# Own terms of a graph layer in SBUF instead of PSUM, and eight low parts moved behind the last one-hots

## The chip, the cores and the metric

The kernel runs on one core of a Trainium2 chip. The metric is the device time in microseconds of one execution. Inputs and outputs are as in the reference; nothing is computed on the host.

## The reference

There are 1250 nodes with 512 features, 20,000 directed edges, and a self loop for each node. A first layer (GIN) sums neighbours, adds the node's own term, and goes through two linear maps with batch norm; a second layer (a hidden map of 256) sums neighbours again. Each is followed by a residual sum and a layer norm.

```
agg = segment_sum(x[src], dst, N)
h = (1 + eps) * x + agg                       # "own term" and sum
h = relu(batch_norm(h @ W1 + b1, g1, be1))    # 512 -> 1024
h = relu(batch_norm(h @ W2 + b2, g2, be2))    # 1024 -> 512
x = layernorm(x + (x + h))
h = relu(x @ V1 + c1) @ V2 + c2               # 512 -> 256 -> 512
x = layernorm(x + (h + segment_sum(h[src], dst, N)))
```

## The kernel before, in words

The five engines have each a program written out by hand in one order, tied by counting semaphores; a wait names the count at which the instruction behind it may go, and everything behind it on that engine waits too. Products in float32 are made of fp32r operands, a high part and a low part (value minus high part), so a product is three matmuls: high by high, high by low, low by high.

The adjacency matrix is never read. VectorE writes one-hot matrices for 50 destination nodes at a time (`one_hots`, lines 850 and 853, 25 groups), TensorE multiplies them into a block of the adjacency (`build`, line 1212), and ScalarE copies the block to `AT` (`group_out`, line 572). TensorE's aggregate (line 1232) multiplies the features by `AT`: twelve sums, numbered i = 0 to 11, four feature blocks for each of three column chunks of 250, 500 and 500 nodes (so sums 0 to 3 have 250 columns, 4 to 11 have 500). Sum i stands in PSUM bank 2 + i % 6. Sums 0 to 3 are accumulated in group slots 0 to 14, sums 4 to 7 in slots 15 to 24, in between the builds, and sums 8 to 11 behind the last group, one after another.

A finished sum goes through three steps. `h0_own(i)` on VectorE (line 864) adds (1 + eps) x to it, and writes back into the bank. `h0_high(i)` on ScalarE (line 597) copies it to `h0h` as fp32r. `h0_low(i)` on VectorE (line 871) writes the difference to `h0l`. For the first eight sums these stand 2, 3 and 5 groups behind the group that ends the sum (`OWN_LAG`, `HIGH_LAG`, `LOW_LAG`), between VectorE's one-hots, and the last of them right behind the last group.

Then VectorE's program goes on: the parameters out of PSUM (line 957), four small multiplications for `gains` (line 961), and then, interleaved, the self loops (`loops(k)`, line 966, k = 0 to 9, an int16 addition into `half_out`) and the steps of sums 8 to 11: loops 0, 1, 2, own 8, loops 3, low 8; loops 4, 5, own 9, loops 6, low 9; loops 7, 8, own 10, loops 9, low 10; own 11, low 11. ScalarE's program beside it: `halve` 0 to 3 (line 642, `AT` rows to int16 in one of four `half_out` buffers), high 8, halve 4, 5, 6, high 9, halve 7, 8, 9, high 10, high 11. SyncE stores each `half_out` behind its `loops` (line 403); `halve(k)` for k of 4 and more waits until the store of k - 4 has landed, since it writes the same buffer. GpSimd at this time subtracts for the low parts of W1 (line 486, eight instructions, two tensors in SBUF read, one written), which begin when the last block of `AT` is copied.

TensorE goes from the last sum straight to the first linear map (line 1296): for output tile t, column chunks c = 0, 1, 2, four feature blocks, three matmuls each. For t = 0 chunk c waits until h0l_set has reached 7, 8 and 12. Tile t = 2 waits until batch norm and activation of tile 0 have freed its banks.

Of the kernel before, what the change touches and what calls it, by code (L numbers as in the profile page):

```python
# [6 lines left out]
F32 = mybir.dt.float32  # L7
# [4 lines left out]
ACT = mybir.ActivationFunctionType  # L12
AX_X = mybir.AxisListType.X

P = 128
# [4 lines left out]
def cdiv(a, b):  # L20
    return -(-a // b)


def gnn_kernel(nc, x, src, dst, eps, w1, b1, g1, be1, w2, b2, g2, be2, lw1, lb1, lw2, lb2, out, a_spill):
# [14 lines left out]
    DT, HT, LT = D // P, H // P, L // P  # L39
# [6 lines left out]
    NG = NW // WG  # L46
# [10 lines left out]
    CH = [(0, 250), (250, 750), (750, 1250)]  # L57
# [5 lines left out]
    with ctx:  # L63
        def sem(name):
            return ctx.enter_context(nc.semaphore(name))
# [10 lines left out]
        R_H0 = R_AT + cdiv(NT * N * 4, 64) * 64  # L76
# [6 lines left out]
        def at(name, shape, dt, offset):  # L83
            return nc.alloc_sbuf_tensor_at(name, shape, dt, offset=offset)
# [13 lines left out]
        def small(n):  # L98
            o = small_n[0]
            small_n[0] += n  # L100
            assert small_n[0] <= SMALL
            return small_t[:, o:o + n]

        xs = at("xs", [P, NT, D], F32, R_W + 32 * KB - NT * D * 4)
        xT = at("xT", [P, DT, N], F32, R_XT + XSHIFT)
# [7 lines left out]
        h0h = [at(f"h0h{c}", [P, DT, c1 - c0], F32R, R_H0 + 2 * DT * c0 * 4) for c, (c0, c1) in enumerate(CH)]  # L113
        h0l = [at(f"h0l{c}", [P, DT, c1 - c0], F32R, R_H0 + DT * (c0 + c1) * 4) for c, (c0, c1) in enumerate(CH)]

        w1s = at("w1s", [P, HT, DT * P], F32, R_W)
        wl = at("wl", [P, HT, DT * P], F32R, R_W)
        wh = at("wh", [P, HT, DT * P], F32R, R_W + 16 * KB)
# [71 lines left out]
        eps_in, asked, eps1 = small(1), small(1), small(1)  # L190
# [32 lines left out]
        ps = ctx.enter_context(nc.psum_tensor("ps", [P, 8, BANK], F32))  # L223
# [6 lines left out]
        x_turned, xT_set, h0_own_set = sem("x_turned"), sem("xT_set"), sem("h0_own_set")  # L230
# [5 lines left out]
        const, ident_set = sem("const"), sem("ident_set")  # L236
# [11 lines left out]
        h0_sum, h0h_set, h0l_set = sem("h0_sum"), sem("h0h_set"), sem("h0l_set")  # L248
# [23 lines left out]
        RING = 6  # L272

        def zbank(t, n):
            return 2 + 3 * (t % 2) + n
# [60 lines left out]
        NI = len(CH) * DT  # L336
# [8 lines left out]
            for j in range(per):  # L345
                slot_units[slots[j * len(slots) // per]].append(units[c * per + j])
        tail_units = units[(len(CH) - 1) * per:]
        OWN_LAG, HIGH_LAG, LOW_LAG = 2, 3, 5
        EARLY = CHG[0]
        cols_at = {6: half + 2, 7: half + 3, 11: half + 4}  # L350
        turn_at = {6: half + 2, 7: half + 3, 12: half + 4}
# [6 lines left out]
        def h0_after(g):  # L358
            return [i for i, k in slot_units[g] if k == NT - 1] if g >= 0 else []
# [200 lines left out]
        def _(act):  # L560
# [30 lines left out]
            def h0_high(i):  # L591
                c, d = divmod(i, DT)
                c0, c1 = CH[c]
                act.wait_ge(h0_own_set, i + 1)
                if i == 0:
                    act.wait_ge(const, 9)
                nc.scalar.activation(h0h[c][:, d, :], ps[:, 2 + i % 6, 0:c1 - c0], ACT.Copy).then_inc(h0h_set, 1)

            for k in range(half):
                x_high(k)  # L600
# [198 lines left out]
        def _(v):  # L799
            n = [0]  # L800

            def link(ins):
# [11 lines left out]
                                           in1=src_i[0:ER, :], op0=ALU.mult, op1=ALU.add).then_inc(pair_set, 1)  # L814
            nc.vector.scalar_tensor_tensor(out=edge_row[0:ER, :], in0=win_row[0:ER, :], scalar=dst_f[0:ER, 0:1],
                                           in1=below[0:ER, :], op0=ALU.is_gt, op1=ALU.subtract).then_inc(rowsel, 1)
# [19 lines left out]
            for c in range(2):  # L836
# [7 lines left out]
                                                    in1=keyT[:, :, c], op0=ALU.add, op1=ALU.subtract))  # L844
# [12 lines left out]
            def h0_own(i):  # L857
                c, d = divmod(i, DT)
                c0, c1 = CH[c]
                v.wait_ge(h0_sum, i + 1)  # L860
                if i == 0:
                    v.wait_ge(xT_set, NT)
                o = ps[:, 2 + i % RING, 0:c1 - c0]
                nc.vector.scalar_tensor_tensor(out=o, in0=xT[:, d, c0:c1], scalar=eps1[:, 0:1], in1=o,
                                               op0=ALU.mult, op1=ALU.add).then_inc(h0_own_set, 1)

            def h0_low(i):
                c, d = divmod(i, DT)
                c0, c1 = CH[c]
                v.wait_ge(h0h_set, i + 1)  # L870
                nc.vector.tensor_tensor(h0l[c][:, d, :], ps[:, 2 + i % 6, 0:c1 - c0],
                                        h0h[c][:, d, :].bitcast(F32), ALU.subtract).then_inc(h0l_set, 1)

            v.wait_ge(const, 7)
# [8 lines left out]
            with v.If(bad == 0):  # L883
                for g in range(EARLY, NG):
                    one_hots(g)
                    if g in low_at:
                        x_low(low_at[g])
                    for i in h0_after(g - OWN_LAG):
                        h0_own(i)
                    for i in h0_after(g - LOW_LAG):  # L890
                        h0_low(i)
                for g in range(NG, NG + LOW_LAG):
                    for i in h0_after(g - OWN_LAG) if g - OWN_LAG < NG else []:
                        h0_own(i)
                    for i in h0_after(g - LOW_LAG):
                        h0_low(i)
            with v.Else():


                v.wait_ge(const, 9)  # L900
                for k in low_at.values():
                    x_low(k)
                v.wait_ge(AT_set, EARLY)
                nc.vector.memset(gen_0[:, :], 0.0).then_inc(gen_zero, 1)
                nc.vector.tensor_copy(gen_src[0:ER, :], src_i[0:ER, :]).then_inc(gen_copied, 1)
                with v.Fori(0, NT) as h:
                    with v.Fori(0, EC) as f:
                        v.wait_ge(gen_copied, h * 4 + 1)

                        v.wait_ge(gen_used, h * (EC + 1) + f + 1)  # L910
                        nc.vector.tensor_scalar(gen_s[0:ER, :], iota2[0:ER, :, 0], gen_src[0:ER, bass.ds(f, 1)],
                                                None, ALU.is_equal).then_inc(gen_hot, 1)
                        nc.vector.tensor_scalar(gen_d[0:ER, :], nodes[0:ER, :], dst_f[0:ER, bass.ds(f, 1)],
                                                None, ALU.is_equal).then_inc(gen_hot, 1)
                    v.wait_ge(gen_sum, h + 1)
                    for c, (c0, c1) in enumerate(CH):
                        nc.vector.tensor_copy(AT[:, bass.ds(h, 1), c0:c1],
                                              ps[:, 2 + c, None, 0:c1 - c0]).then_inc(gen_copied, 1)
                    nc.vector.tensor_scalar(gen_src[0:ER, :], gen_src[0:ER, :], -float(P), None,
                                            ALU.add).then_inc(gen_copied, 1)  # L920
                v.wait_ge(gen_copied, 4 * NT + 1)
                nc.vector.memset(n_out[:, :], 0.0).then_inc(AT_set, NG - EARLY)
                for i in range(NI - DT):
                    h0_own(i)
                    h0_low(i)


            def row_stats(k, part):
# [233 lines left out]
        def _(pe):  # L1162
# [53 lines left out]
            def aggregate(i, k):  # L1216
                c, d = divmod(i, DT)
                c0, c1 = CH[c]
                o = ps[:, 2 + i % RING, 0:c1 - c0]
                if k == 0:  # L1220
                    pe.wait_ge(AT_set, CHG[c])
                    if i >= RING:
                        pe.wait_ge(h0l_set, i - RING + 1)
                    elif i >= DT:
                        pe.wait_ge(xT_set, NT)
                    else:
                        pe.wait_ge(xT_set, half)
                if i == 0:
                    pe.wait_ge(xl_set, k + 1)
                r = rows[k]  # L1230
                for j, part in enumerate((xh, xl)):
                    last = mm(o, part[0:r, k, d * P:d * P + P], AT[0:r, k, c0:c1], start=(k == 0 and j == 0),  # L1232
                              stop=(k == NT - 1 and j == 1))
                if k == NT - 1:
                    last.then_inc(h0_sum, 1)
# [51 lines left out]
            for t in range(HT):  # L1287
                pe.wait_ge(w1l_set, t + 1)
                if t >= 2:
                    pe.wait_ge(act_set, 2 * t - 2)  # L1290
                for c, (c0, c1) in enumerate(CH):
                    if t == 0:
                        pe.wait_ge(h0l_set, max(DT * (c + 1), 7 + c))
                    for d in range(DT):
                        for j, (w, h) in enumerate(((wh, h0h), (wl, h0h), (wh, h0l))):
                            last = mm(ps[:, zbank(t, c), 0:c1 - c0], w[:, t, d * P:d * P + P], h[c][:, d, :],  # L1296
                                      start=(d == 0 and j == 0), stop=(d == DT - 1 and j == 2))
                        if c == len(CH) - 1 and d == DT - 1:
                            last.then_inc(z_sum, 1)
# [137 lines left out]
```

## Time and profile before

| what | value |
|---|---|
| median of 3 runs | 249.21 us (248.9 to 249.46) |
| the profiled execution, its own time | 249.12 us |
| its span, first to last instruction | 247.1 us |
| TensorE matmul busy | 231.4 us, 94% of the span |
| VectorE, ScalarE, GpSimd busy | 156.2, 134.2, 87.5 us |
| share of TensorE in the chain that ended last | 69% |
| mean granted TensorE clock | 0.992 |

Times in a trace are from the first instruction of the span. The profiled execution's own time is 2.0 us longer than its span, which is what lies around the span. A busy share says little about a stretch: what counts in a stretch is which wait ends last there. "Idle before" of an instruction is the time for which its engine stood still ahead of it.

### The profile page before, as it was taken

The numbers are of one execution on the slowest core, as the hardware profiler recorded it, in microseconds if no ns is written. First come the engines' busy times: TensorE is split into PE (matmuls) and PEld (weight loads), VectorE is DVE, ScalarE is ACT, GpSimd is POOL, SyncE is SP. The second block draws the span as 40 slices with busy tenths as digits, with TensorE's granted clock in tenths as the row PEclk, the third lists the DMA queues.
The fourth block names the chain that finished last, engine by engine and source line by source line (L and its number), as shares of the span: only waits on it lengthen the run. The fifth ranks groups of instructions, "written<-read, shape, count | busy, mean of one in ns | idle before, by whom it ended". The sixth has DMA issues, their size and how long they took to land.

```text
span 247.1 us, 3901 instructions
## 1 busy us (share of the span) xinstructions
PE 231.4 (94%) x1454; PEld 197.8 (80%) x1454; DVE 156.2 (63%) x362; ACT 134.2 (54%) x233; POOL 87.5 (35%) x83
## 2 busy tenths in 40 slices
PE   1859999999999999999999999999999999999991
PEld 1738988777888878888888888888889997888970
DVE  2778999873965343555554326164786899796274
ACT  0936865664677067444445504457461639935373
POOL 7500000006900007565654500423366459701241
PEclk9997999999999999999999999999999999999999
DMA  5287600000086401111000098503209920000334
GB/s 176 88 265 198 163 0 3 1 3 3 3 311 232 157 1 45 42 42 45 0 0 0 0 201 153 106 3 69 38 9 164 209 78 3 0 0 0 131 126 161
DMA packets 32322, 19.96 MB, mean 81 GB/s; under 512 B 21927, under 2 KB 27084, under 8 KB 32302
## 3 DMA queue, kind: packets, MB, share of 16 engines
q1 hardware_dynamic: 31868, 19.47, 29.7%
q8 instruction: 13, 0.21, 0.4%
q0 software_dynamic: 160, 0.13, 0.2%
q10 hardware_dynamic: 274, 0.09, 0.1%
q14 instruction: 7, 0.06, 0.1%
HBM read 8.51 MB, written 5.92 MB: 58 GB/s over the span
## 4 chain that ended last, share of the span: by engine, by line
PE 69%; DVE 12%; ACT 7%; DMA 5%; issue 2%; POOL 2%; SPq 1%; DVEq 0%; POOLq 0%; ACTq 0%
PE ps L1296 19%; PE ps L1232 17%; PE ps L1313 11%; PE ps L1359 9%; PE ps L1377 6%; PE ps L1326 3%; DMA plane_T<-planes 2%; PE ps L1212 2%; DVE small_t L943 2%; DVE xT L987 2%; DVE hot_s L850 2%; DMA pairs<-pair 1%; ACT planes L718 1%; DMA run<-pairs,start_i 1%; ACT a L681 1%
## 5 line engine op out<-in xcount | busy, mean ns | idle before, releaser
L943 DVE BATCH_NORM_STATS2 small_t<-ps 128x6 f32<-128x500 f32 (+1 forms) x36 | 21.6, 599 | 39.1 <-PE ps L1296 25.6
L1232 PE MATMUL ps<-AT,xh 128*128 128x500 f32 (+2 forms) x120 | 42.7, 367 | 0.2 <-ACT AT L572 0.2
L1232 PE MATMUL ps<-AT,xl 128*128 128x500 f32 (+2 forms) x120 | 40.9, 352 | 0.0
L1296 PE MATMUL ps<-h0h,wh 128*128 128x500 f32 (+1 forms) x96 | 33.9, 353 | 0.2 <-ACT a L681 0.2
L1296 PE MATMUL ps<-h0h,wl 128*128 128x500 f32 (+1 forms) x96 | 33.9, 353 | 0.0
L1296 PE MATMUL ps<-h0l,wh 128*128 128x500 f32 (+1 forms) x96 | 33.8, 352 | 0.0
L491 POOL TENSOR_TENSOR wl<-w2s,wh 128x512 fp32r<-128x512 f32 x8 | 11.1, 1382 | 44.4 <-ACT wh L692 44.4
L486 POOL TENSOR_TENSOR wl<-w1s,wh 128x512 fp32r<-128x512 f32 x8 | 10.1, 1296 | 45.8 <-ACT AT L572 45.8
L1232 PEld LDWEIGHTS ps<-AT,xh 128*128 128x128 f32 (+1 forms) x120 | 22.6, 188 | 3.2 <-ACT AT L572 0.4
L1232 PEld LDWEIGHTS ps<-AT,xl 128*128 128x128 f32 (+1 forms) x120 | 22.7, 189 | 2.7
L1313 PE MATMUL ps<-a1h,wh 128*128 128x500 f32 (+1 forms) x96 | 23.7, 355 | 0.0
L1313 PE MATMUL ps<-a1h,wl 128*128 128x500 f32 (+1 forms) x96 | 23.5, 353 | 0.0
L1313 PE MATMUL ps<-a1l,wh 128*128 128x500 f32 (+1 forms) x96 | 23.4, 353 | 0.0
L572 ACT ACTIVATE AT<-ps 128x500 fp32r<-128x500 f32 x25 | 14.7, 589 | 15.4 <-PE ps L1212 15.4
L850 DVE TENSOR_TENSOR hot_s<-iota,loT 128x1280 bf16<-128x1280 bf16 x25 | 20.5, 819 | 2.4 <-PE ps L1212 2.2
L1359 PE MATMUL ps<-A,uh 128*128 128x512 f32 (+3 forms) x60 | 20.5, 357 | 0.0
L1296 PEld LDWEIGHTS ps<-h0h,wh 128*128 128x128 f32 x96 | 18.1, 188 | 3.0 <-issue 0.6
L1359 PE MATMUL ps<-A,ul 128*128 128x512 f32 (+3 forms) x60 | 20.3, 354 | 0.0
L1296 PEld LDWEIGHTS ps<-h0l,wh 128*128 128x128 f32 x96 | 18.0, 188 | 2.5
L1296 PEld LDWEIGHTS ps<-h0h,wl 128*128 128x128 f32 x96 | 18.1, 188 | 2.4
L495 POOL TENSOR_TENSOR a1l<-a,a1h 128x1250 fp32r<-128x1250 f32 x7 | 18.8, 2681 | 0.0
L666 ACT ACTIVATE small_t<-small_t 128x1 f32<-128x1 f32 x12 | 3.5, 295 | 27.7 <-DVE small_t L944 27.6
(150 smaller groups left out, 509.2 us busy)
## 6 DMA issues: line engine op xcount, KB each, us to landing
turns<-half_out SPq DMA_DIRECT2D x10, 320.0 KB, 2.2
out<-x SPq DMA_DIRECT2D x9, 256.0 KB
w1s<-in_L_gnn_W SPq DMA_DIRECT2D x4, 512.0 KB, 7.0
w2s<-in_L_gnn_W SPq DMA_DIRECT2D x8, 256.0 KB, 2.8
xs<-in_x SPq DMA_DIRECT2D x1, 1280.0 KB, 6.4
xs<-in_x SPq DMA_DIRECT2D x1, 1024.0 KB
lws<-in_L_gnn_W SPq DMA_DIRECT2D x1, 512.0 KB, 3.9
lw2s<-in_L_gnn_W SPq DMA_DIRECT2D x1, 512.0 KB, 4.3
```

The costliest lines, as they stand in the source:

```text
L486: nc.gpsimd.tensor_tensor(wl[:, t, :], w1s[:, t, :], wh[:, t, :].bitcast(F32), ALU.subtract).then_inc(w1l_set, 1)
L491: nc.gpsimd.tensor_tensor(wl[:, t, :], w2s[t % W2R][:, :], wh[:, t, :].bitcast(F32), ALU.subtract).then_inc(w2l_set, 1)
L495: nc.gpsimd.tensor_tensor(a1(a1l, t), a32[t % 2][:, :], a1(a1h, t).bitcast(F32), ALU.subtract).then_inc(a1l_set, 1)
L572: nc.scalar.activation(AT[:, :, g * WG * WIN:(g + 1) * WG * WIN].rearrange("p k (w d) -> p k w d", w=WG), ps[:, g % 2, 0:GCOLS].rearrange( ...
L850: nc.vector.tensor_tensor(hot_s[g % 2][:, :, :, :], iota2[:, None, :, :].broadcast_to([P, WG, P, 2]), loT[:, w, None, :].broadcast_to([P, ...
L943: link(nc.vector.bn_stats(stats[:, 6 * c:6 * c + 6], ps[:, zbank(t, c), 0:c1 - c0]))
L1232: last = mm(o, part[0:r, k, d * P:d * P + P], AT[0:r, k, c0:c1], start=(k == 0 and j == 0), stop=(k == NT - 1 and j == 1))
L1296: last = mm(ps[:, zbank(t, c), 0:c1 - c0], w[:, t, d * P:d * P + P], h[c][:, d, :], start=(d == 0 and j == 0), stop=(d == DT - 1 and j == 2))
L1313: last = mm(ps[:, zbank(t, c), 0:c1 - c0], w[:, k, (t - HT) * P:(t - HT + 1) * P], a1(a, k)[:, c0:c1], start=(k == 0 and j == 0), stop=(k ...
L1326: last = mm(u_at(k), x[:, d, P * k:P * k + r], w[:, d, :], start=(d == 0 and j == 0 and k % 2 == 0), stop=(d == DT - 1 and j == 2), skip_g ...
L1359: last = mm(v_at(i, m), (uh, ul)[j][0:r, k, m * P:m * P + P], a_rows(k)[0:r, c0:c1], start=(k == 0 and j == 0 and (m == 0 or v_banks[i][0] ...
L1377: last = mm(ps[0:r, y_banks[k % len(y_banks)], :], part[:, f:f + r], w[:, m, :], start=(m == 0 and j == 0), stop=(m == LT - 1 and j == 2))
```

## The change

`h0_own` writes its result to `h0f`, a float32 view in SBUF of the place of `h0l`. `h0_high` and `h0_low` read it from there, `h0_low` in place. The aggregate's wait for a free bank counts own terms and no longer low parts, and the first linear map has an added wait on own terms for its banks. The low parts 0 to 7 leave VectorE's loop over the groups and stand together behind own 7, ahead of the copy of the parameters. Sums 8 to 11 keep their order.

```diff
+        h0f = [at(f"h0f{c}", [P, DT, c1 - c0], F32, R_H0 + DT * (c0 + c1) * 4) for c, (c0, c1) in enumerate(CH)]
...
-        OWN_LAG, HIGH_LAG, LOW_LAG = 2, 3, 5
+        OWN_LAG, HIGH_LAG = 2, 3
...
                 act.wait_ge(h0_own_set, i + 1)
-                if i == 0:
-                    act.wait_ge(const, 9)
-                nc.scalar.activation(h0h[c][:, d, :], ps[:, 2 + i % 6, 0:c1 - c0], ACT.Copy).then_inc(h0h_set, 1)
+                nc.scalar.activation(h0h[c][:, d, :], h0f[c][:, d, :], ACT.Copy).then_inc(h0h_set, 1)
...
                 if i == 0:
                     v.wait_ge(xT_set, NT)
-                o = ps[:, 2 + i % RING, 0:c1 - c0]
-                nc.vector.scalar_tensor_tensor(out=o, in0=xT[:, d, c0:c1], scalar=eps1[:, 0:1], in1=o,
+                    v.wait_ge(const, 9)
+                nc.vector.scalar_tensor_tensor(out=h0f[c][:, d, :], in0=xT[:, d, c0:c1], scalar=eps1[:, 0:1],
+                                               in1=ps[:, 2 + i % RING, 0:c1 - c0],
                                                op0=ALU.mult, op1=ALU.add).then_inc(h0_own_set, 1)
...
                 v.wait_ge(h0h_set, i + 1)
-                nc.vector.tensor_tensor(h0l[c][:, d, :], ps[:, 2 + i % 6, 0:c1 - c0],
+                nc.vector.tensor_tensor(h0l[c][:, d, :], h0f[c][:, d, :],
                                         h0h[c][:, d, :].bitcast(F32), ALU.subtract).then_inc(h0l_set, 1)
...
                     for i in h0_after(g - OWN_LAG):
                         h0_own(i)
-                    for i in h0_after(g - LOW_LAG):
-                        h0_low(i)
-                for g in range(NG, NG + LOW_LAG):
-                    for i in h0_after(g - OWN_LAG) if g - OWN_LAG < NG else []:
+                for g in range(NG - OWN_LAG, NG):
+                    for i in h0_after(g):
                         h0_own(i)
-                    for i in h0_after(g - LOW_LAG):
-                        h0_low(i)
...
                 for i in range(NI - DT):
                     h0_own(i)
-                    h0_low(i)
+            for i in range(NI - DT):
+                h0_low(i)
...
                     if i >= RING:
-                        pe.wait_ge(h0l_set, i - RING + 1)
+                        pe.wait_ge(h0_own_set, i - RING + 1)
...
                     if t == 0:
                         pe.wait_ge(h0l_set, max(DT * (c + 1), 7 + c))
+                        pe.wait_ge(h0_own_set, 7 + c)
```

## Rows read from the trace of the kernel before

**Rows 1.** The page: busy time, share of the span and instructions.

```profile
PE 231.4 (94%) x1454; PEld 197.8 (80%) x1454; DVE 156.2 (63%) x362; ACT 134.2 (54%) x233; POOL 87.5 (35%) x83
```

**Rows 2.** The chain that ended last, in order of time: start, us, what.

```profile
59.44 18.38 PE ps L1232 x80
77.82 6.87 PE ps L1296 x36
...
91.68 41.27 PE ps L1296 x216
```

**Rows 3.** Windows view of the group loop: length, busy us of each engine, clock.

```profile
37.76:59.26 21.50, 21.50 (x172) 16.47 (x171) 15.26 (x31) 12.53 (x25) 1.19 (x1) 1.00 0.01 3
```

**Rows 4.** Timeline of VectorE from 43 to 81 us: start, us, instruction.

```profile
43.88 1.38 DVE L871 TENSOR_TENSOR h0l<-ps,h0h 128x250 fp32r<-128x250 f32 x4
...
50.12 0.67 DVE L871 TENSOR_TENSOR h0l<-ps,h0h 128x500 fp32r<-128x500 f32 x1
...
59.30 0.74 DVE L864 SCALAR_TENSOR_TENSOR ps<-xT,small_t,ps 128x500 f32<-128x500 f32 x1 [3.86 <-PE ps L1232]
59.95 1.43 DVE L871 TENSOR_TENSOR h0l<-ps,h0h 128x500 fp32r<-128x500 f32 x2
...
61.52 4.14 DVE L961 TENSOR_SCALAR gains<-small_t 128x8 f32<-128x8 f32 x4
65.69 2.83 DVE L966 TENSOR_TENSOR half_out<-half_out,ident 128x128 int16<-128x128 int16 x3
68.44 0.73 DVE L864 SCALAR_TENSOR_TENSOR ps<-xT,small_t,ps 128x500 f32<-128x500 f32 x1
...
80.11 0.68 DVE L871 TENSOR_TENSOR h0l<-ps,h0h 128x500 fp32r<-128x500 f32 x1 [0.66 <-ACT h0h L597]
```

**Rows 5.** Timeline of TensorE: the first matmul of chunk 2 of tile 0, and of tile 1.

```profile
81.79 0.39 PE L1296 MATMUL ps<-h0h,wh 128*128 128x500 f32 x1
...
84.52 0.28 PE L1296 MATMUL ps<-h0h,wh 128*128 128x250 f32 x1
```

**Rows 6.** Timeline of GpSimd behind the last group.

```profile
58.07 10.10 POOL L486 TENSOR_TENSOR wl<-w1s,wh 128x512 fp32r<-128x512 f32 x8 [45.80 <-ACT AT L572]
```

**Rows 7.** Timelines of VectorE and GpSimd where two instructions overlap, in two places.

```profile
139.51 1.46 DVE L982 TENSOR_TENSOR a1l<-a,a1h 128x1250 fp32r<-128x1250 f32 x1 [2.99 <-ACT a1h L701]
140.08 2.04 POOL L491 TENSOR_TENSOR wl<-w2s,wh 128x512 fp32r<-128x512 f32 x1 [2.71 <-ACT wh L692]
...
170.83 2.89 POOL L503 TENSOR_TENSOR xpl<-xT,xph 128x1250 fp32r<-128x1250 f32 x1 [8.17 <-ACT xph L709]
171.73 3.08 DVE L1002 TENSOR_TENSOR lw1l<-lws,lw1h 128x1024 fp32r<-128x1024 f32 x1 [3.40 <-ACT lw1h L728]
```

**Rows 8.** Groups by form, VectorE: busy us and mean ns of one.

```profile
L1033 DVE TENSOR_TENSOR xpl<-xT,xph 128x500 fp32r<-128x500 f32 x1 | 0.7, 671 | 0.0
L953 DVE TENSOR_SCALAR small_t<-gains,small_t 128x1 f32<-128x1 f32 x24 | 5.1, 214 | 1.0 <-DVE small_t L948 0.2
```

**Rows 9.** Timeline of SyncE's queue, and the landing times of line 403.

```profile
67.09 11.19 SPq L403 DMA_DIRECT2D turns<-half_out  x10
...
DMA to landing us min/median/max: 2.2/2.2/2.8
```

**Rows 10.** Timeline of ScalarE: halve 4.

```profile
69.69 1.24 ACT L642 ACTIVATE half_out<-AT 128x1250 int16<-128x1250 f32 x1
```

**Rows 11.** Timelines at 212 us: VectorE's first line 1104, GpSimd's two instructions beside it.

```profile
211.96 3.57 DVE L1104 SCALAR_TENSOR_TENSOR x<-b_all,small_t,x 128x512 f32<-128x512 f32 x1 [1.52 <-ACT x L747]
...
211.38 1.23 POOL L529 CAST A<-half_in 98x1250 fp32r<-98x1250 int16 x1
212.58 2.40 POOL L551 TENSOR_TENSOR lw2l<-lw2s,lw2h 128x1024 fp32r<-128x1024 f32 x1
```

**Rows 12.** Windows view of TensorE: length, PE busy, granted clock, DMA share, GB/s.

```profile
12.00:17.70 5.70, 2.51 (x29) 1.00 0.80 247
17.70:21.10 3.40, 3.38 (x40) 0.50 0.44 117
```

## The prediction

> **What bounds the kernel now.** The page comes first: TensorE is busy 94% of the span [rows 1], so a gain must come from a stretch in which TensorE waits. The windows view shows that there is none where the change takes work away: in the 21.50 us of the group loop in which low parts stand, TensorE is busy for 21.50 [rows 3]. The chain in order of time says the same for what follows: 80 matmuls of sums 8 to 11, then the 36 of tile 0 without a wait between them, then batch norm and activation of tile 0, and only when that has freed the banks the 216 of tiles 2 to 7 [rows 2]. From this the reader should keep two things. Up to 84.7 us only a wait that is new can move TensorE. And a wait ahead of the end of tile 0 is not made up for: tile 1 takes as long as tile 0, 6.9 us, and from tile 0's end at 84.7 to tile 2's start at 91.68 is 7.0 us, the chain's own length.
>
> The engine's timelines come next, for the margin. The last matmuls of tile 0, chunk 2, start at 81.79 [rows 5] and need low part 11, which ends at 80.11 + 0.68 = 80.79 [rows 4]. The margin is 1.0 us. Own 8 starts at 68.44, and from there to 80.79 own, high and low parts, halves and self loops wait for each other in turn, 12.35 us.
>
> **What it removes.** Four low parts of 250 columns (1.38 us) and two of 500 columns (0.67 each, the second like the one shown) leave VectorE's loop, 2.7 us [rows 4]. Low parts 6 and 7 were behind own 7 already. Gain: nothing, as TensorE had no wait there [rows 3], and VectorE itself then idles for 3.86 us ahead of own 7, which waits for the sum [rows 4]. The bounds are 0 and 0.5 us, the latter what a faster pitch of the matmuls could give (a rival, below). The bank waits that now count own terms were met long before. Writing the own term to SBUF, and reading it from there on ScalarE: no row shows the same form with the other memory; the nearest, a subtraction of 500 columns with all in SBUF, takes 0.671 us [rows 8] against 0.67 to 0.68 from PSUM [rows 4]. I take zero, with bounds of 0.1 us either way.
>
> **What it adds: eight low parts behind own 7, and now each reads two tensors in SBUF.** They stand ahead of the parameters, the four instructions of `gains`, self loops 0 to 2 and own 8. Alone they would be cheap. But GpSimd is at its eight subtractions, 58.07 to 68.17, 1.26 us each [rows 6], and the trace shows that such pairs exclude each other. At 171.73 a VectorE subtraction of 1024 columns, both inputs in SBUF, took 3.08 us; at the rate of the 500-column one (0.671) and the 1250-column one (1.46), 1.05 ns a column, it should take 1.2. It ended 1.09 us after GpSimd's instruction (170.83 + 2.89 = 173.72), so it stood until that was done. At 140.08 it is GpSimd that took 2.04 in place of 1.26, and ended 1.15 us after VectorE's [rows 7, 8]. The old low parts, with one input in PSUM, show nothing of this: two of them in 1.43 us while GpSimd worked [rows 4, 6].
>
> The Trainium skill (SBUF — State Buffer, § Who interferes with whom) states the rule: a VectorE instruction with two SBUF inputs takes its second one through the read interface that GpSimd reads by, and whichever comes second is blocked for the whole instruction. By this rule the low parts are new rivals of GpSimd, and without it they would cost the time of the case "no exclusion" below; these rows agree with it.
>
> Who goes next when both have a queue? `gains` needed 4.14 us for four tiny instructions, one per GpSimd instruction, and GpSimd still had work until 68.17: one got in behind each of GpSimd's [rows 4, 6]. I take this turn-taking. A blocked low part then ends 0.27 us (250 columns) or 0.53 us (500) after GpSimd's instruction, and the next of GpSimd's 1.15 us later:
> - GpSimd's second ends at 60.6. Four low parts of 250 with GpSimd's next behind each: 4 x 1.42 = 5.7, 66.3.
> - Two of 500 with GpSimd's seventh and eighth: 2 x 1.68 = 3.4, 69.7. GpSimd is done (its w1 parts are needed from 77.8 on, so its own delay costs nothing).
> - Two more of 500: 0.53 + 0.6, 70.8.
> - Parameters 0.2, and `gains` now unhindered, 4 x 0.25 by the 214 ns of line 953 and its gap [rows 8]: 72.0.
> - Self loops 0 to 2, 0.2 each (alone): loops 0 ends at 72.3, own 8 starts at 72.6, 4.2 late.
>
> What is queued behind it: high 8 when own 8 is done, 0.73 later, and halve 4, which was at 69.69 [rows 10]. It needs store 0 landed as well. The first store was issued at 67.09, 0.1 after loops 0, and lands 2.2 us later [rows 9]: now 72.4 + 2.2 = 74.6. So the store, not own 8, sets halve 4: 4.9 late. The rest of the 12.35 us shifts with it, low part 11 ends at 85.7, and TensorE, which can do chunks 0 and 1 and no more, waits 4.9 - 1.0 = about 4.0 us (rounding kept upward for the semaphore). SyncE's loads of W2, behind the stores in its queue, move from 78.4 to 83.3; ScalarE takes the first of them behind the activation of tile 0, which ended by 91.68 [rows 2], so they cost nothing.
>
> **What a stall costs beyond itself.** In 12.00 to 17.70 TensorE was busy for 2.51 of 5.70 us, and then the granted clock was 0.50 for 3.4 us, the 1.2 GHz level [rows 12]. The new gap of 4 us may bring the same, just ahead of the rest of tile 0. If 3.4 us at the half level are all work, 1.7 us are lost; if part of them falls into the gap, less. I take 1.5, with bounds 0 and 1.7.
>
> **Sum.** 249.12 (the profiled execution's own time, 0.1 below the median) + 4.0 + 1.5 = 254.6 us.
>
> **Rivals.**
> - *GpSimd first.* At 211.96 a VectorE instruction with two SBUF inputs took 3.57 us: it waited for a cast and for the subtraction that followed it too [rows 11]. If low part 0 had so to wait until 68.17: eight low parts unhindered, 0.27 + 3 x 0.35 + 4 x 0.6 = 3.7 (0.35 from 1.38 / 4, rows 4), to 71.9, `gains` to 73.1, loops 0 to 73.4, landing 75.7, halve 4 6.0 late, stall 5.0; with 0 to 1.7 of clock 254.1 to 255.8. Against it stands `gains`, in this very stretch.
> - *VectorE keeps its turn.* All eight in one go: 60.6 to 64.3, GpSimd's other six until 71.9. `gains` and two self loops wait for one each, own 8 at about 72.0, 3.5 late; store 0 landed in time. Stall 2.5: 251.6, with the clock 253.1. For it: low parts have no wait between them, `gains` had.
> - *No exclusion.* The low parts run from 59.95 to 63.7 beside GpSimd; `gains` still waits four times, to 68.2; loops 0 at 68.4 in place of 67.0, its store landed at 70.7, halve 4 1.0 to 1.2 late, stall 0.0 to 0.2: 249.1 to 249.3, no change. Rows 7 speak against it.
> - *Faster.* The loop's matmuls share PSUM with fewer readers and writers. A matmul of sums 8 to 11 takes 18.38 / 80 = 0.2298 us [rows 2], while the 12 of chunk 2, beside an almost idle VectorE, take (84.52 - 81.79) / 12 = 0.2275 [rows 5]; over the 160 long matmuls of sums 4 to 11 that is 0.4 us, 248.8. It decides only if halve 4 is at most 1.0 us late, hence only without exclusion.
>
> **Chances.** Turn-taking with the clock falling 0.42, without it (253.1) 0.13; GpSimd first 0.12; VectorE keeps its turn 0.15; no exclusion 0.08; faster 0.05; a stall longer than any of these, say by a store that lands after 2.8 us and two low clock stretches, 0.05. The range 251.6 to 256.2 holds the first four. What this kernel's timing can tell from no change is about 0.2%, 0.5 us: faster 0.05, same 0.08, slower 0.87.
>
> **What the profile after would show.** Low parts 0 to 7 on VectorE from 59.95 to about 70.8, some of them near 1.4 to 1.8 us long, and line 486 on GpSimd stretched beyond 10.10 us; `gains` at 0.2 to 0.4 us each; the first store at about 72.4; on TensorE a gap of about 4 us ahead of chunk 2 of tile 0, at 81.8, put down to the low part of line 871; perhaps a clock of 0.5 behind it; and from tile 2 to the end the same lengths as before. I am wrong if line 486 keeps its 1.26 us and the low parts their 0.4 and 0.67, or if the margin at 81.8 is larger than I read it.

## The result, and the profile after

The changed kernel takes 254.68 us (median of 5 runs) against 248.9 (median of 5) for the kernel before on the same chip; the ratio is 1.0241, 95% interval 1.020 to 1.028: slower by 2.4%. Forecast were 254.6 us and slower. One run of the changed kernel, 330.86 us, was disturbed and stands outside the ratio. In a second measurement on another chip the changed kernel takes 254.61 against 249.04, ratio 1.0245 (1.0206 to 1.0284).

The profiled execution took 257.7 us, 3 us more than the median. Most of that, some 2.5 us, has a cause ahead of the change, so it is set apart first; the rest, 0.9 us, is a longer stretch at the lower clock, shown further down. This is the piece of the changed kernel's chain that differs:

```profile
4.69 6.49 DMA pairs<-pair
```

The same transfer took 3.70 us in the kernel before's profile. Everything behind it in the profile below is late for that reason: own 7 starts at 61.62, 2.32 us after its place in [rows 4]. A second profiled execution of the changed kernel, 254.45 us, from the second measurement, had no such delay (the transfer took 3.63 us, own 7 started at 59.12), and the accounts below are made with it.

VectorE's timeline of the changed kernel, where [rows 4] show the one before:

```profile
61.62 0.73 DVE L863 SCALAR_TENSOR_TENSOR h0f<-xT,small_t,ps 128x500 f32<-128x500 f32 x1 [4.45 <-PE ps L1229]
62.27 10.86 DVE L871 TENSOR_TENSOR h0l<-h0f,h0h 128x250 fp32r<-128x250 f32 x8
73.05 0.18 DVE L954 COPY small_t<-ps 128x36 f32<-128x36 f32 x1
73.27 0.79 DVE L958 TENSOR_SCALAR gains<-small_t 128x8 f32<-128x8 f32 x4
74.09 0.70 DVE L963 TENSOR_TENSOR half_out<-half_out,ident 128x128 int16<-128x128 int16 x3
74.71 0.73 DVE L863 SCALAR_TENSOR_TENSOR h0f<-xT,small_t,ps 128x500 f32<-128x500 f32 x1
...
87.26 0.68 DVE L871 TENSOR_TENSOR h0l<-h0f,h0h 128x500 fp32r<-128x500 f32 x1 [0.69 <-ACT h0h L596]
```

The eight low parts take 10.86 us where the forecast reckons 3.7 for eight alone. `gains`, which waited for GpSimd four times (4.14 us), now takes 0.79: GpSimd is through by then. GpSimd's and SyncE's timelines, against [rows 6] and [rows 9]:

```profile
60.39 11.62 POOL L487 TENSOR_TENSOR wl<-w1s,wh 128x512 fp32r<-128x512 f32 x8 [45.68 <-ACT AT L573]
...
74.46 10.89 SPq L404 DMA_DIRECT2D turns<-half_out  x10
```

Line 487 is stretched from 10.10 to 11.62 us. The length of one, by the view of that line and of line 871 (ns min/median/max):

```profile
L487 POOL TENSOR_TENSOR wl<-w1s,wh x8: 1288/1465/1728, 60.4 to 70.3; 128x512 fp32r<-128x512 f32 x8
...
L871 DVE TENSOR_TENSOR h0l<-h0f,h0h x12: 667/1214/1767, 62.3 to 87.3; 128x500 fp32r<-128x500 f32 x8, 128x250 fp32r<-128x250 f32 x4
```

The shortest of GpSimd, 1288, is the length without a wait, and so is 667 for a low part of 500 columns; the longest are 1728 and 1767. The store and TensorE follow. First ScalarE's timeline, against [rows 10], then TensorE's, against [rows 5]:

```profile
75.47 0.62 ACT L596 ACTIVATE h0h<-h0f 128x500 fp32r<-128x500 f32 x1 [7.54 <-DVE h0f L863]
76.71 1.25 ACT L641 ACTIVATE half_out<-AT 128x1250 int16<-128x1250 f32 x1 [0.62 <-DMA turns<-half_out]
```

```profile
83.89 0.39 PE L1294 MATMUL ps<-h0l,wh 128*128 128x500 f32 x1
87.99 0.78 PE L1294 MATMUL ps<-h0h,wh 128*128 128x500 f32 x1 [3.71 <-DVE h0l L871]
```

Halve 4 is put down to the store, 0.62 us after high 8 was done. On TensorE the next matmul would start 0.23 after the one at 83.89, at 84.12; it starts at 87.99, a gap of 3.87 us, put down to a low part. Behind it the windows view shows the lower level of the clock, 1.2 GHz, and then the upper:

```profile
87.10:93.80 6.70, 5.81 (x16) 0.50 0.41 152
93.90:120.00 26.10, 26.10 (x139) 1.00 0.11 31
```

In the second profiled execution the chain from the low parts to the first map reads so, times from the start of its own span:

```profile
59.78 10.86 DVE h0l L871 x8
...
71.60 0.31 DVE half_out L963
...
71.97 2.23 DMA turns<-half_out
...
74.22 3.80 ACT half_out L641 x6
...
84.77 0.69 DVE h0l L871
...
85.50 52.63 PE ps L1294 x264
138.13 2.08 PE ps L1311 x11
```

Low parts, self loop 0, the store, halve 4 to 6, and so to low part 11: that is the forecast's path, engine by engine. The account: chunk 2 starts at 85.50 in place of 81.79, 3.71 later (a gap of 3.89 less 0.18 by which TensorE was early in this execution). From there to the second map it is 52.63 us, and 51.15 before (from 81.79 in [rows 5] to the end of the 216 matmuls in [rows 2], 132.94): 1.48 for the clock. Together 5.19; the spans differ by 252.4 - 247.1 = 5.3, the times by 254.45 - 249.12 = 5.3. Nothing of size is left for the rest of the kernel.

### The profile page after: what moved, and what is told of

It is laid out like the page before. It is cut to its first block, busy times and chain, and to the rows that moved or that the text cites. A ratio compares the mean times of both kernels' runs of the same rounds, so it can differ in the third digit from the quotient of the medians.

```text
span 255.7 us, 3902 instructions
## 1 busy us (share of the span) xinstructions
PE 233.9 (91%) x1454; PEld 199.3 (78%) x1454; DVE 157.6 (62%) x362; ACT 134.7 (53%) x233; POOL 89.0 (35%) x83
## 4 chain that ended last, share of the span: by engine, by line
PE 61%; DVE 17%; ACT 9%; DMA 8%; issue 2%; POOL 1%; SPq 1%; DVEq 0%
PE ps L1294 21%; PE ps L1311 11%; PE ps L1357 9%; PE ps L1229 9%; PE ps L1375 5%; DVE h0l L871 5%; ACT half_out L641 3%; PE ps L1324 3%; DVE hot_s L849 3%; DMA pairs<-pair 3%; DMA plane_T<-planes 2%; PE ps L1209 2%; DVE xT L984 2%; ACT planes L717 1%; DVE small_t L940 1%
## 5 line engine op out<-in xcount | busy, mean ns | idle before, releaser
L1294 PE MATMUL ps<-h0h,wh 128*128 128x500 f32 (+1 forms) x96 | 35.1, 365 | 3.7 <-DVE h0l L871 3.7
L1294 PE MATMUL ps<-h0h,wl 128*128 128x500 f32 (+1 forms) x96 | 34.9, 364 | 0.0
L1294 PE MATMUL ps<-h0l,wh 128*128 128x500 f32 (+1 forms) x96 | 34.9, 363 | 0.0
L487 POOL TENSOR_TENSOR wl<-w1s,wh 128x512 fp32r<-128x512 f32 x8 | 11.6, 1486 | 45.7 <-ACT AT L573 45.7
L1294 PEld LDWEIGHTS ps<-h0h,wh 128*128 128x128 f32 x96 | 18.9, 196 | 6.8 <-DVE h0l L871 4.1
L1294 PEld LDWEIGHTS ps<-h0l,wh 128*128 128x128 f32 x96 | 18.8, 195 | 2.7
L1294 PEld LDWEIGHTS ps<-h0h,wl 128*128 128x128 f32 x96 | 18.8, 196 | 2.6
```

The source lines that it names most:

```text
L487: nc.gpsimd.tensor_tensor(wl[:, t, :], w1s[:, t, :], wh[:, t, :].bitcast(F32), ALU.subtract).then_inc(w1l_set, 1)
```

## The experiments

Two theories of the lateness were to be told apart: the low parts and GpSimd's subtractions exclude each other since both inputs of a low part stand in SBUF; or it is the move alone, eight instructions in front of everything that sum 8 waits for. Beside them stand the terms of the sum: the store, the gap, the clock. The first four kernels ran on one chip, where the kernel before had a median of 249.49 (25 runs, from 248.7 to 252.25), the last four on another, median 249.04 (15 runs). Each profile's times count from its own start.

**GpSimd held back.** Line 485:

```diff
             pl.wait_ge(AT_set, NG)
+            pl.wait_ge(h0_own_set, 9)
```

> The changed kernel, with GpSimd's eight W1 subtractions held back until own 8 is done. Theory (VectorE's low parts and GpSimd's subtractions exclude each other, and that makes own 8 late): the eight low parts run from own 7 on in about 3.7 us at 0.41 and 0.67 us each, gains takes about 1 us, own 8 starts some 7 us earlier than in the changed kernel, TensorE has no gap ahead of chunk 2 of tile 0, time 248.9 (within 0.3) as the kernel before. Rival (it is the 3.7 us of low parts in front of own 8, whatever GpSimd does, with the store behind it): low parts keep their lengths of 0.9 to 1.8 us and the time stays near 254.4.

Measured: ratio 1.0028 (0.9983 to 1.0073), no difference from the kernel before; median 250.34, five of ten runs from 248.77 to 249.56 and five from 251.12 to 251.62 (the kernel before on this chip has two such clusters too, see the last section). VectorE's timeline:

```profile
60.15 3.76 DVE L872 TENSOR_TENSOR h0l<-h0f,h0h 128x250 fp32r<-128x250 f32 x8
63.83 0.19 DVE L955 COPY small_t<-ps 128x36 f32<-128x36 f32 x1
64.05 0.79 DVE L959 TENSOR_SCALAR gains<-small_t 128x8 f32<-128x8 f32 x4
...
65.49 0.73 DVE L864 SCALAR_TENSOR_TENSOR h0f<-xT,small_t,ps 128x500 f32<-128x500 f32 x1
...
66.90 1.28 DVE L872 TENSOR_TENSOR h0l<-h0f,h0h 128x500 fp32r<-128x500 f32 x1 [0.49 <-ACT h0h L597]
```

The same eight instructions at the same place take 3.76 us, not 10.86. Low part 8, now beside GpSimd, takes 1.28 in place of 0.68. TensorE has no gap ahead of chunk 2, and the whole loss is gone. But holding GpSimd back also takes `gains` from 4.14 to 0.79 us, about as much as the low parts add. So this does not yet show that the move by itself costs nothing, nor that two SBUF inputs are what makes it dear.

**One SBUF input.** Low parts 0 to 7 subtract from PSUM bank 1 in place of `h0f`, so that they are not those of the reference. The added wait, for the last block of `AT`, was met before they began:

```diff
-                nc.vector.tensor_tensor(h0l[c][:, d, :], h0f[c][:, d, :],
+                other = ps[:, 1, 0:c1 - c0] if i < NI - DT else h0f[c][:, d, :]
+                nc.vector.tensor_tensor(h0l[c][:, d, :], other,
                                         h0h[c][:, d, :].bitcast(F32), ALU.subtract).then_inc(h0l_set, 1)
...
+            v.wait_ge(AT_set, NG)
             for i in range(NI - DT):
```

> The changed kernel, with low parts 0 to 7 subtracting from a block of PSUM bank 1 in place of h0f: one SBUF input in place of two, same place, same size, same count; the low parts of these eight sums are then not those of the reference. Theory (exclusion by the second SBUF input): they take 0.41 and 0.67 us each though GpSimd works beside them, GpSimd keeps 1.26 us each, gains still waits four times, the first store is issued about 1.3 us later than before, TensorE's gap is 0 to 0.3 us, time 248.9 to 249.3. Rival (the move itself, 3.7 us of work ahead of gains and own 8, or SBUF as output): a gap of 2.5 to 4 us and 252 to 254.4.

Measured: ratio 1.0003 (0.9958 to 1.0048), no difference. Its profile, with the same slow first transfer as above and hence about 3 us late, on VectorE, GpSimd and TensorE:

```profile
63.19 3.73 DVE L872 TENSOR_TENSOR h0l<-ps,h0h 128x250 fp32r<-128x250 f32 x8
...
67.05 4.33 DVE L960 TENSOR_SCALAR gains<-small_t 128x8 f32<-128x8 f32 x4
...
61.30 10.06 POOL L487 TENSOR_TENSOR wl<-w1s,wh 128x512 fp32r<-128x512 f32 x8 [46.33 <-ACT AT L573]
...
84.80 0.39 PE L1296 MATMUL ps<-h0l,wh 128*128 128x500 f32 x1
85.31 0.50 PE L1296 MATMUL ps<-h0h,wh 128*128 128x500 f32 x1
```

This settles it. GpSimd works beside the low parts, at 10.06 us unhindered, and they are unhindered too, 3.73. One input's memory is different, with place, count, size and output the same. (The low parts are then no longer in place either. That being in place is what blocks is ruled out by [rows 7]: line 1002, which is not in place, stood until GpSimd was done.) `gains` waits its four times as before, 4.33 us. Reckoned as above, the gap ahead of chunk 2 is 85.31 - (84.80 + 0.23) = 0.28 us: the 3.7 us of work moved in front of own 8 cost about that much, for in the kernel before `gains` and loops 0 and 1 waited for GpSimd until 68.2, and here GpSimd is done soon after `gains` (71.36), so that the loops run free (0.70 us for three in place of 2.83).

One thing stays open. `gains` reads a single tensor in SBUF and waits for GpSimd all the same. So it is shown for this subtraction, with its other input in PSUM, that it is free beside GpSimd; it is not shown for every VectorE instruction with one SBUF input.

**Work in the gap.** Sixteen matmuls of 500 columns into the unused bank 1, ahead of chunk 2 of tile 0:

```diff
                 for c, (c0, c1) in enumerate(CH):
+                    if t == 0 and c == len(CH) - 1:
+                        for _ in range(16):
+                            mm(ps[:, 1, 0:BANK - 12], wh[:, 0, 0:P], h0h[1][:, 0, :], start=True, stop=True)
                     if t == 0:
```

> The changed kernel, with 16 matmuls of 500 columns into the unused PSUM bank 1 between chunk 1 and chunk 2 of tile 0, 3.6 us of work inside the gap of 3.9. Theory (the gap costs its own length, and the lower clock behind it another 1.5 to 2.4 us): the clock stays at 1.00 through 96 us, a gap of about 0.3 us is left, and the time falls to 248.9 + 3.9 = 252.8. Rival (the clock term is not on the path, the gap is all): the time stays at 254.4.

Measured: ratio 1.0164 (1.0083 to 1.0244), median 253.06 of four runs. That interval alone would also allow the rival's 254.4 (a ratio of 1.020); the traces decide. The windows view, around the start of chunk 2 at 85.49, of this kernel and then of the changed one without the filler (second execution):

```profile
81.00:85.40 4.40, 4.38 (x20) 1.00 0.82 285
85.50:89.10 3.60, 3.60 (x19) 1.00 0.54 199
```

```profile
85.80:89.10 3.30, 3.30 (x9) 0.50 0.54 196
```

Chunk 2 starts at 85.49 here and at 85.50 there; the chain to the second map is 51.09 us here and 52.63 there. The low clock behind the gap costs 1.5 us, and work that nobody needs gives it back. What is left, chunk 2 at 85.49 in place of 81.79, 3.7 us, is the gap itself.

**Low parts 0 to 5 back in the loop.**

```diff
-        OWN_LAG, HIGH_LAG = 2, 3
+        OWN_LAG, HIGH_LAG, LOW_LAG = 2, 3, 5
...
-                for g in range(NG - OWN_LAG, NG):
-                    for i in h0_after(g):
+                    for i in h0_after(g - LOW_LAG):
+                        h0_low(i)
+                for g in range(NG, NG + LOW_LAG):
+                    for i in h0_after(g - OWN_LAG) if g - OWN_LAG < NG else []:
                         h0_own(i)
+                    for i in h0_after(g - LOW_LAG):
+                        h0_low(i)
...
                 for i in range(NI - DT):
                     h0_own(i)
-            for i in range(NI - DT):
-                h0_low(i)
+                    h0_low(i)
```

> The changed kernel with low parts 0 to 5 back at their old places in the group loop: own terms still in SBUF, but only low parts 6 and 7 behind own 7. Theory: these two wait for GpSimd and hold it, 1.4 to 1.8 us each in place of 0.67, gains waits four times more; own 8 about 1.1 us late, the first store 2 us late, halve 4 about 1.7 us late, gap 0.7 us, no fall of the clock, time 249.6 (249.2 to 250.2). Rival (the own term in SBUF costs by itself, the place of the low parts does not matter): near 254.4. Rival (only the number of low parts behind own 7 matters, not the exclusion): 248.9.

Measured: median 250.44 of ten runs, 249.94 to 250.65 but for one, above the 249.2 to 250.2 that I expected; ratio 1.0022 (0.9975 to 1.0068), which is too wide for so small a loss. The profile shows it: TensorE's timeline at chunk 2 has

```profile
81.53 0.39 PE L1297 MATMUL ps<-h0l,wh 128*128 128x500 f32 x1
82.72 0.50 PE L1297 MATMUL ps<-h0h,wh 128*128 128x500 f32 x1 [0.79 <-DVE h0l L871]
```

and store 0 is issued at 69.20, 2.1 us late; halve 4 starts at 71.43, 1.7 late, both as expected. Two low parts in place of eight behind own 7 leave a gap of 0.96 us, reckoned as above (82.72 - 81.53 - 0.23), where 0.7 was expected, and no fall of the clock behind it. Half of that miss, 0.13 us, is ScalarE's reading from SBUF (next section). Both rivals are out: the time is far from 254.4, and a gap is there.

**The changed kernel again,** as reference of the next three.

> The changed kernel again, on the chip of the next three, as their reference. All theories: 5.5 us above the kernel before.

Measured: 254.61 against 249.04, 5.6 us.

**Self loops first.** Low parts 0 to 7 go behind self loops 0 to 2, ahead of own 8:

```diff
-            for i in range(NI - DT):
-                h0_low(i)
...
                     loops(k)
+                if j == 0:
+                    for i in range(NI - DT):
+                        h0_low(i)
                 h0_own(NI - DT + j)
```

> The changed kernel with low parts 0 to 7 moved behind gains and self loops 0 to 2, directly ahead of own 8, so that the first store is as early as in the kernel before and GpSimd is through before they begin. Theory: gains and two self loops wait for GpSimd's third to eighth subtraction, the low parts then run unhindered in 3.7 us, own 8 and halve 4 are both about 3.8 us late (no store to wait for), gap 2.9 us in place of 3.9; time 2.9 plus 0 to 1.7 us of lower clock above the kernel before, about 1 us below the changed kernel. Rival (the store is not what sets halve 4, the sum of VectorE's work is): the gap stays 3.9 and the time is that of the changed kernel. Rival (exclusion is all, and the 3.7 us of work nothing): no gap, time as before.

Measured: 253.51, ratio 1.0177 (1.0153 to 1.0201), 1.1 us below the changed kernel. VectorE, then ScalarE and TensorE:

```profile
60.64 4.22 DVE L956 TENSOR_SCALAR gains<-small_t 128x8 f32<-128x8 f32 x4
64.90 3.94 DVE L961 TENSOR_TENSOR half_out<-half_out,ident 128x128 int16<-128x128 int16 x3
68.76 3.75 DVE L871 TENSOR_TENSOR h0l<-h0f,h0h 128x250 fp32r<-128x250 f32 x8
72.44 0.72 DVE L863 SCALAR_TENSOR_TENSOR h0f<-xT,small_t,ps 128x500 f32<-128x500 f32 x1
...
73.72 1.23 ACT L641 ACTIVATE half_out<-AT 128x1250 int16<-128x1250 f32 x1
...
82.03 0.39 PE L1295 MATMUL ps<-h0l,wh 128*128 128x500 f32 x1
85.00 0.78 PE L1295 MATMUL ps<-h0h,wh 128*128 128x500 f32 x1 [2.57 <-DVE h0l L871]
```

Own 7 starts at 59.77 here and at 59.12 in the changed kernel's second execution. Reckoned from it, own 8 starts after 12.67 us, and in the changed kernel (72.21) after 13.09: 0.4 apart. Halve 4 starts after 13.95 and 15.10 (74.22): 1.15 apart. The 0.7 between are the store's. The gap is 2.74 us (85.00 - 82.03 - 0.23), with 2.9 expected, and the clock fell behind it too: from 85.00 to the second map it is 52.43 us, 1.3 more than before. The low parts are unhindered and still cost 3.75 us, as they now stand behind `gains` and loops that have waited for GpSimd. So neither of the two places behind own 7 is free while GpSimd is at work.

**Low parts 0 to 6 ahead of own 7,** in VectorE's idle time:

```diff
-                for g in range(NG - OWN_LAG, NG):
-                    for i in h0_after(g):
-                        h0_own(i)
+                for i in range(NI - DT - 1):
+                    h0_low(i)
+                h0_own(NI - DT - 1)
+                h0_low(NI - DT - 1)
...
                 for i in range(NI - DT):
                     h0_own(i)
-            for i in range(NI - DT):
-                h0_low(i)
+                    h0_low(i)
```

> The changed kernel with low parts 0 to 6 ahead of own 7, into the 4 us in which VectorE waits for sum 7; only low part 7 stays behind own 7. Theory: low parts 0 to 5 are done before GpSimd starts at 58, low part 6 may wait for its first subtraction, low part 7 waits once; gains four times as before; first store about 1.9 us late, halve 4 1.3 late, gap 0.3 to 0.5 us, time 0.2 to 0.8 us above the kernel before. Rival (own terms in SBUF make low parts dear wherever they stand): near the changed kernel.

Measured: 250.23, ratio 1.0061 (1.0038 to 1.0084), 1.2 us above the kernel before and outside what I expected. VectorE:

```profile
54.70 2.58 DVE L871 TENSOR_TENSOR h0l<-h0f,h0h 128x250 fp32r<-128x250 f32 x6
58.46 1.37 DVE L871 TENSOR_TENSOR h0l<-h0f,h0h 128x500 fp32r<-128x500 f32 x1 [1.17 <-ACT h0h L596]
59.74 0.72 DVE L863 SCALAR_TENSOR_TENSOR h0f<-xT,small_t,ps 128x500 f32<-128x500 f32 x1
61.16 1.61 DVE L871 TENSOR_TENSOR h0l<-h0f,h0h 128x500 fp32r<-128x500 f32 x1 [0.69 <-ACT h0h L596]
```

Six low parts are indeed free. The other two meet GpSimd, and each also holds it back (two of its eight take 1.74 us in place of 1.29), which `gains`, one wait for each of GpSimd's instructions, then hands on: own 8 at 69.40, store 0 at 69.14, 2.05 late, halve 4 at 71.38, 1.7 late in place of 1.3, gap 0.94 in place of 0.3 to 0.5. I had counted the waits of VectorE and left out that GpSimd's end moves as well.

**The same with GpSimd held back,** as in the first experiment:

> The same with GpSimd's W1 subtractions held back until own 8 is done. Theory: no pair of instructions excludes another until own 8, which starts as soon as sum 8 is there (about 64) and gains are done; no gap on TensorE; time as the kernel before, within 0.3, and not below it, since TensorE has no wait left in this stretch to give back. Rival (VectorE's and ScalarE's earlier end frees something): more than 0.3 us below the kernel before.

Measured: 249.12, ratio 1.0016 (0.9992 to 1.0041), same as before. Own 8 starts at 65.03 in place of 68.44 and TensorE has no gap ahead of chunk 2. Nothing comes of the 3.4 us, as TensorE was busy throughout already. So no version beats the kernel before; this one equals it with the own terms in SBUF.

## Why the prediction was right

- **No gain from the loop.** Right. TensorE's loop has the same 1.90 + 0.28 us per group, and the two kernels with GpSimd held back, whose VectorE is done early, are not faster.
- **Own terms in SBUF cost nothing.** Nearly right: 0.73 us on VectorE before and after. But ScalarE's copy takes 0.62 in place of 0.59, and three copies stand between halve 4 and low part 11. From the start of one to the start of the other it was 10.42 us (69.69 to 80.11) and is 10.55 (74.22 to 84.77), and 10.54 to 10.56 in the five experiments in which halve 4 is on the way to a gap. So 0.13 us, taken as zero with a bound of 0.1, is part of the gap.
- **Two SBUF inputs exclude GpSimd's subtractions.** Right, and shown by the one-input kernel. It agrees with the rule of the Trainium skill (SBUF — State Buffer, § Who interferes with whom). Blocked low parts started 1.43 us apart (250 columns) and 1.69 (500), where the terms of the sum were 1.42 and 1.68 per turn.
- **Turn-taking.** Right: GpSimd's were stretched by turns (1.46 and 1.73), so neither engine ran all of its queue first. Low parts 10.86 us, forecast 59.95 to 70.8, 10.9.
- **Own 8 4.2 late, the store sets halve 4 at 4.9 late.** In the second execution own 8 is at 72.21, 3.8 late, and halve 4 at 74.22, 4.5 late. Reckoned from own 7, which was 0.18 us earlier there, they are 4.0 and 4.7 late. `gains` and the loops were a little quicker than forecast. The self-loops-first kernel gives the store 0.7 us, as the forecast had it (4.9 - 4.2).
- **Gap 4.0.** Measured 3.9. That it comes so near is in part luck: halve 4 was 0.2 us less late than forecast, and the stretch behind it 0.13 longer, which nearly cancel.
- **Clock 1.5.** 1.5 in one profiled execution, 2.4 in the other (53.55 - 51.15), which is past the bound of 1.7: there the lower level lasted 6.8 us, not 3.4. That bound was too narrow; that the gap can bring down two such stretches I had only in the case of 0.05.
- **Sum 5.5 above the kernel before.** Measured 5.6 and 5.8 in the medians, 5.3 in the second profiled execution. The case that VectorE keeps its turn, GpSimd first and no exclusion are refuted by the lengths of lines 487 and 871; faster, by the time. Why in [rows 11] a VectorE instruction let two of GpSimd's pass before it, while here one of each went in turn, no experiment tried.

## What to carry to other kernels

Ahead of moving an operand from PSUM to SBUF, look at what GpSimd does at that time: a two-input subtraction on VectorE that had one input in PSUM was free beside it, and with both in SBUF eight of them took 10.9 us in place of 3.7, and held GpSimd back too. Count in both directions, as everything that waits in turn hands the delay on. And price a new gap on a full TensorE at its length plus, if it is long enough, the slower clock behind it (1.3 to 2.4 us here behind gaps of 2.7 and 3.9 us, nothing behind gaps of 1.0 and less); filling it with idle matmuls gives back only the second part.

## What the hardware showed that was not expected

- The first transfer on the chain (`pairs`, 83 KB, written while 1280 KB of x were loaded) takes 3.6 to 3.8 us in eight of the ten profiled executions, and 6.49 and 6.67 in the other two (the changed kernel's first and the one-input kernel's); everything follows it. Of the 25 runs of the kernel before in the first set 16 lie from 248.70 to 249.64 and 9 from 250.65 to 252.25, a second cluster by about that distance. That it is this transfer in each of them was not profiled, and why it takes two lengths stays open.
- After the same gap of 3.9 us the clock was at 0.50 for 3.4 us in one execution and for 6.8 in another, with 1.5 and 2.4 us lost. The gap of 2.7 brought it down for 3.4 us, with 1.3 lost. After gaps of 0.96, 0.94 and 0.28, and the 0.23 left behind the filler, it did not fall. Why the stretch was twice as long in one execution stays open.
- A store's landing of 2.2 us set halve 4 wherever loops 0 ended only 0.3 us before own 8 started, so also with GpSimd held back (67.48), where nothing came of it. It is a wait that no row of the kernel before names, since there it ended 0.4 us ahead of halve 4's start (67.09 + 2.2 against 69.69).
